# Projecting keys and values of all batches in a stage of their own, and stacking the halves of two heads in 64 rows each by the loads

## The reference, cut to what matters

```python
q = x @ Wq.T + bq;  k = context @ Wk.T + bk;  v = context @ Wv.T + bv     # 256 columns = 16 heads of 16
attn = softmax(einsum('bihd,bjhd->bhij', q, k) * 16 ** -0.5)              # 112 queries, 375 keys
out = einsum('bhij,bjhd->bihd', attn, v).reshape(B, NQ, 256)
return out @ Wo.T + bo
```

## Time and profile before

| | us |
|---|---|
| median of 3 runs (lowest to highest) | 3871.93 (3871.74 to 3872.47) |
| the profiled execution | 3868.77 |
| its span | 3867.0 |
| PE busy | 3016.1 (78%) |
| VectorE, ScalarE, POOL busy | 1709.9, 1316.2, 905.7 |

### The profile page before, as it was taken

How to read it: one execution, slowest core, us unless ns; L and a number is a source line. 1 busy time by engine, 2 the same in 40 slices (tenths; PEclk the granted TensorE clock), 3 DMA queues, 4 the chain that set the end, 5 groups by cost and what they waited for, 6 DMA issues and landing times. The chain is left out here.

```text
span 3867.0 us, 59553 instructions
## 1 busy us (share of the span) xinstructions
PE 3016.1 (78%) x19704; PEld 2381.5 (62%) x19704; DVE 1709.9 (44%) x3313; ACT 1316.2 (34%) x2657; POOL 905.7 (23%) x934
## 2 busy tenths in 40 slices
PE   4999929999999820999993588788888888709980
PEld 2666618777778710888882355466676667608870
DVE  2444467666667532000003444465655556502323
ACT  1222245555555300333330222344444445302220
POOL 0000004433334150000004100232323333160015
PEclk7999959999999755999996789899999999759995
DMA  4000000000000233565552000000000000035653
GB/s 109 1 1 0 0 9 13 14 13 16 13 14 13 96 102 97 170 199 190 182 199 88 19 0 0 12 13 14 10 13 10 13 7 13 1 92 182 202 171 113
DMA packets 174569, 234.68 MB, mean 61 GB/s; under 512 B 25184, under 2 KB 141376, under 8 KB 174384
## 3 DMA queue, kind: packets, MB, share of 16 engines
q1 hardware_dynamic: 156496, 184.23, 15.4%
q0 software_dynamic: 17888, 47.73, 3.7%
HBM read 186.04 MB, written 45.88 MB: 60 GB/s over the span
## 5 line engine op out<-in xcount | busy, mean ns | idle before, releaser
L1214 POOL TENSOR_TENSOR x_qH<-x_q_high,head_mask 128x448 fp32r<-128x448 f32 x256 | 277.0, 1082 | 1580.3 <-DVE x_q_low L1271 1246.4
L1284 DVE TENSOR_REDUCE x_neg_max<-banks 112x2 f32<-112x750 f32 x512 | 456.3, 933 | 259.7 <-PE banks L998 259.6
L1156 ACT ACTIVATE x_probT<-banks 125x448 f32<-125x448 f32 x768 | 417.1, 543 | 420.4 <-PE banks L1018 412.0
L1014 PE MATMUL banks<-x_qH,x_kS 128*125 128x448 f32 x768 | 383.5, 499 | 34.9 <-issue 32.4
L1734 PE MATMUL banks<-f_xT,f_w 128*128 128x256 f32 x1680 | 386.2, 385 | 17.6 <-DMA f_w<-in_L_ffn_w 12.9
L1746 PE MATMUL banks<-f_w,f_hT 128*128 128x256 f32 x1680 | 374.2, 379 | 0.0
L1734 PEld LDWEIGHTS banks<-f_xT,f_w 128*128 128x128 f32 x1680 | 319.6, 192 | 76.3 <-issue 23.2
L1746 PEld LDWEIGHTS banks<-f_w,f_hT 128*128 128x128 f32 x1680 | 313.9, 190 | 39.9
L1018 PE MATMUL banks<-x_diag,x_ones 112*125 112x448 f32 x768 | 288.9, 376 | 0.0
L1016 PE MATMUL banks<-x_qL,x_kS 128*125 128x448 f32 x768 | 288.2, 375 | 0.0
L970 PE MATMUL banks<-x_ctxT,x_wk 128*128 128x375 f32 x512 | 203.7, 522 | 83.0 <-DVE x_o L1302 79.9
(11 more groups left out here) (271 smaller groups left out, 4989.0 us busy)
## 6 DMA issues: line engine op xcount, KB each, us to landing
f_w<-in_L_ffn_w SPq DMA_DIRECT2D x70, 1024.0 KB, 8.3
f_w<-in_L_ffn_w SPq DMA_DIRECT2D x70, 512.0 KB, 5.0
f_x_slots<-slot_x SPq DMA_DIRECT2D x70, 256.0 KB, 6.0
slot_y<-f_y POOLq DMA_DIRECT2D x70, 256.0 KB, 5.5
f_ctx_rows<-in_ctx SPq DMA_DIRECT2D x32, 281.2 KB
x_cnat<-in_ctx SPq DMA_DIRECT2D x32, 281.2 KB
slot_x<-f_zero SPq DMA_DIRECT2D x10, 896.0 KB, 11.6
x_ctxT<-in_ctx_T SPq DMA_DIRECT2D x32, 187.5 KB
```

Source lines behind the costliest of these rows:

```text
L1014: pe.matmul(to, kS[:, r, q, keys], qH[:, r, heads, :].rearrange("p h t -> p (h t)"), start=True, stop=False)
L1156: act.activation(probT[:, u % 2, c].rearrange("k h t -> k (h t)"), ST[i % 2][0:KB, 0:HU * T], ACT.Exp).then_inc(exp_done, 1)
L1214: pool.tensor_tensor(qH[:, r, to, :], wide(q_high[:, q:q + 1, :], 1, HU), mask, ALU.mult).then_inc(qH_ready, 1)
L1284: dve.tensor_reduce(mx[:, u % 2, 2 * pair:2 * pair + 2], psum[0:T, 2 * pair:2 * pair + 2, 0:NKV], AX_X, ALU.max, negate=True).then_inc(max ...
```

## The change

There are eight stages: before each cross attention a new `project_context(e, layer)` goes through all batches, makes the keys and the value rows, and stores them in DRAM (`k_halves`: per batch, head half and high or low part, 128 rows of 376; `v_rows`: per batch 125 rows of 1536). In it each slot pair of batches has its own buffers, keys are cut straight out of PSUM by ScalarE (high) and VectorE (rest), and SP issues, in order, two stores of one batch and the load of another. The columns of the weights are reordered so that a head's 16 numbers come as rows `d * 8 + pair`.

In the cross attention two heads now share the 128 rows, 64 each: `kP` has for a head pair, per head, high, low, high, low of 16 rows each, and `qP` high, high, low, low against it, with zeros in the other head's 64 rows (zeroed once). So one pass gives all four products of the parts, and the masks of POOL and the second tile of queries are gone. The stacking is done by the loads: `load_keys` issues four DMAs a batch (two halves of the pairs x two heads), each reading 32 rows twice (`wide(..., 0, 2)`) into 64 partitions; the query parts are stored to DRAM (`store_query`) and read back by `load_query` with four DMAs, each 16 rows twice into 32 partitions. `load_values` reads the value rows. An exponent is the matmul of ones with the diagonal (448 columns) and one matmul a head pair (224 columns). Scores run two units ahead instead of one, one pair in each of a unit's first two slots, and the query is made two batches ahead.

```diff
+        env.k_halves = nc.dram_tensor("k_halves", [B, 2, 2, P, NKV + 1], F32, kind="Internal").ap()
+        env.v_rows = nc.dram_tensor("v_rows", [B, KB, NJ * XH * P // XU], F32, kind="Internal").ap()
+        env.q_halves = nc.dram_tensor("q_halves", [2, 2, 2, P, T], F32, kind="Internal").ap()
-        stages = [self_attention, lambda e: cross_attention(e, 0), lambda e: experts(e, 0),
-                  gated_attention, lambda e: cross_attention(e, 1), lambda e: experts(e, 1)]
+        stages = [self_attention, lambda e: project_context(e, 0), lambda e: cross_attention(e, 0),
+                  lambda e: experts(e, 0), gated_attention, lambda e: project_context(e, 1),
+                  lambda e: cross_attention(e, 1), lambda e: experts(e, 1)]
...
+def project_context(e, layer):
...
+                def load(b, i, r):
+                    if layer == 0:
+                        sp.wait_ge(v2_ps, ONE + least(i * 2 + r - 1))
+                        sp.dma_start(ctxT[:, r, 0, :], d["ctx_T"][0:P, bass.ds(b, 1), :].rearrange(
+                            "c b k -> c (b k)")).then_inc(ctx_loaded[r], 16)
+                        sp.dma_start(ctxT[0:C1, r, 1, :], d["ctx_T"][P:DC, bass.ds(b, 1), :].rearrange(
+                            "c b k -> c (b k)")).then_inc(ctx_loaded[r], 16)
+                    else:
+                        sp.wait_ge(cT_ps, ONE + least(i * 4 + 2 * r - 2))
+                        sp.dma_start(cnat[:, r, :, 0:DC], d["ctx_768"][bass.ds(b, 1)].rearrange(
+                            "b (j p) c -> p (b j) c", p=KB)).then_inc(ctx_loaded[r], 16)
...
+                def store(b, i, r):
+                    sp.wait_ge(k_low, ONE + i * 4 + 2 * r + 2)
+                    sp.dma_start(e.k_halves[bass.ds(b, 1)].rearrange("b h l p n -> p (b h l) n"),
+                                 halves[:, r].rearrange("p h l n -> p (h l) n").bitcast(F32)).then_inc(k_stored[r], 16)
+                    sp.wait_ge(v01_ready, ONE + i * 2 + r + 1)
+                    sp.wait_ge(v2_ready, ONE + i * 2 + r + 1)
+                    sp.dma_start(e.v_rows[bass.ds(b, 1)].rearrange("b p n -> p (b n)"),
+                                 v[:, r].rearrange("p c h e -> p (c h e)")).then_inc(v_stored[r], 16)
...
+                with sp.Fori(1, B // 2) as i:
+                    for r in range(2):
+                        store(i * 2 + r - 2, i - 1, r)
+                        load(i * 2 + r, i, r)
...
+    AHEAD = 2
+    RING = 4
+    AT = {"xT": 1, "q": 2, "back": 4, "oT": 7, "y": 8}
...
+                def load_keys(g, s):
...
+                    sp.wait_ge(st_ps, ONE + since(g, NU * NJ, SS * (s - 1)))
+                    parts = e.k_halves[bass.ds(b, 1)].rearrange("b h l (d p) n -> (b h) (l d) (p n)", d=HD)
+                    for half in range(2):
+                        pairs = slice(half * PAIRS // 2, (half + 1) * PAIRS // 2)
+                        keys = slice(pairs.start * (NKV + 1), pairs.stop * (NKV + 1))
+                        for h in range(2):
+                            sp.dma_start(kP[h * HALF:(h + 1) * HALF, r, pairs, :].bitcast(F32),
+                                         wide(parts[h:h + 1, :, keys], 0, 2)).then_inc(k_loaded[half][r], 16)
...
+                def load_query(g, s):
+                    r = s % 2
+                    sp.wait_ge(q_stored[r], g * (8 * GROUP) + 16 * (s // 2 + 1))
+                    parts = e.q_halves[r].rearrange("h l (d p) t -> h l d (p t)", d=HD)
+                    for h in range(2):
+                        for l in range(2):
+                            at = h * HALF + 2 * l * HD
+                            sp.dma_start(qP[at:at + 2 * HD, r, h].rearrange("q p t -> q (p t)").bitcast(F32),
+                                         wide(parts[h, l:l + 1], 0, 2)).then_inc(q_loaded[r], 16)
...
+                        if s < GROUP - 1 or not last:
+                            load_keys(g, s + 1)
+                            load_query(g, s + 1)
+                            load_values(g, s + 1)
+                        if s < GROUP - 2 or not last:
+                            store_query(g, s + 2)
...
-                    pe.matmul(to, kS[:, r, q, keys], qH[:, r, heads, :].rearrange("p h t -> p (h t)"),
-                              start=True, stop=False)
-                    pe.matmul(to, kS[:, r, q, keys], qL[:, r, heads, :].rearrange("p h t -> p (h t)"),
-                              start=False, stop=False)
-                    pe.matmul(to, ones[:], diag[:, u % 2].rearrange("t h k -> t (h k)"), start=False, stop=True)\
-                      .then_inc(st_ps, 1)
+                    pe.matmul(to, ones[:], diag[:, u % RING].rearrange("t h k -> t (h k)"), start=True, stop=False)
+                    for pair in range(2):
+                        last = pe.matmul(to[:, 2 * pair * T:2 * (pair + 1) * T].rearrange("k (h t) -> k h t", t=T),
+                                         kP[:, r, 2 * q + pair, keys],
+                                         qP[:, r, :, 2 * q + pair, :],
+                                         start=False, stop=(pair == 1))
+                    last.then_inc(st_ps, 1)
...
-                        if c == 0 and (u + 1 < NU or not last):
-                            score(g, u + 1, 0)
-                            score(g, u + 1, 1)
+                        if c < 2 and (u + AHEAD < NU or not last):
+                            score(g, u + AHEAD, c)
```

More of the change, by code:

```diff
@@ new lines, in group @@
+                def group(g, is_first, last):
+                    for s in range(GROUP):
+                        if s < GROUP - 1 or not last:
[4 more added lines that the diff above has]
+                            store_query(g, s + 2)
+                load_keys(0, 0)
+                load_values(0, 0)
+                store_query(0, 0)
@@ L1179, in group @@
                         j = SLOT.get(at)
-                        if j in MAKE and (s < GROUP - 1 or not last):
-                            copies(g, s + 1, j)
-                        for k in HIGH:
-                            if at == HIGH[k] and (s < GROUP - 1 or not last):
-                                high(g, s + 1, k)
-                        if j == "oT" and (s >= 1 or not is_first):
+                        if j == "xT" and (s < GROUP - 2 or not last):
+                            copy_xT(g, s + 2)
+                        if j == "oT" and layer == 0 and (s >= 1 or not is_first):
                             copy_oT(g, s - 1)
@@ L1191, in group @@
                             copy_oT(g, GROUP - 1)
-                if layer == 0:
-                    act.wait_ge(e.later, e.later_n)
-                for j in MAKE:
-                    copies(0, 0, j)
-                    if j in HIGH:
-                        high(0, 0, j)
+                for s in range(2):
+                    copy_xT(0, s)
                 all_groups(act, group)
@@ L1221, in group @@
                 def group(g, is_first, last):
-                    for s in range(GROUP - 1 if last else GROUP):
-                        spread(g, s + 1)
-                spread(0, 0)
+                    for s in range(GROUP - 2 if last else GROUP):
+                        add_post(g, s + 2)
+                add_post(0, 0)
+                add_post(0, 1)
                 all_groups(pool, group)
@@ L1340, in group @@
                                 normalise(g, s - 1)
[L1341 removed]
+                            if j == "y" and layer == 0:
                                 add_y(g, s - 1)
```

604 lines of the change are left out of this document (310 added, 294 removed).

## The result

| | us |
|---|---|
| kernel before, median (lowest to highest) | 3872.2 (3871.74 to 3872.59) |
| changed kernel, median (lowest to highest) | 6284.1 (6280.64 to 6292.77) |
| ratio (95% interval) | 1.623 (1.620 to 1.626) |
| span of the profiled execution of the changed kernel | 6282.2 |

The account below looks back on a forecast made before the run. PE's instruction stream was taken to bound both cross attentions before, and loads on two engines after. 2223 us kept, 766 of projection and 3164 of attention gave 6153 us of span, rounded to 6160 us measured, range 5750 to 6780.

Parts of the forecast that it names:

- Two engines for eight transfers: Cross attention: all eight key and query loads, leading count 2, run on the same two engines, 38.3 us a batch.
- rival of sixteen engines: Cross attention: the copies use all sixteen engines, 4.8 us a transfer, some 16 us a batch, 4110 us in all; chance 6%.
- Where the transfer lies: Cross attention: loads hide behind two units only; PE's work behind the wait adds 8.5 us a batch (layer 0), 7 (layer 1).
- The size of the transfer: Cross attention: a batch's key and query loads take 2.5 us of latency plus 38.3 us for 2.00 MB.
- Projection: New projection stages: 10.5 us a batch in layer 0 and 12.5 in layer 1, 766 us in all.
- the chain: Projection stages: PE, evictions, issue, values, load and latency in order over two batches, 8.2 to 10.9 us a batch.
- Work removed from PE: Cross attention: of PE's 23.0 us a batch 14.4 stay in layer 0, of 26.7 in layer 1 15.0 stay.
- A pass of 224 columns: Exponents of cross attention: each narrower PE pass takes 0.11 us; the rival at the upper bound had 1%.
- The rest: Everything outside the projection and cross attention stages: 2223 us stay of the 3867.0 us span.
- faster: Copies and value rows both spread over all engines: attention at 14.4 and 15.0 us a batch, 3754 us; chance 4%.
- no change: Whole kernel: the faster case with 16 us a batch of attention and 530 us of projection, 3867 us; chance 2%.
- The other signs: Attention: some 50 GB/s, PE busy about a quarter, period 48 to 50 us, longest waits on `qP`, clock near 0.6.

Follow-up runs that it names:

- copies_inside: Changed kernel with the copy loads' repeat moved inside the rows for keys, and query loads reading high and low once: ratio 1.056, 4161.5 us.
- values_128: Changed kernel with value rows padded by three rows of zeros, stored and loaded as 128 rows instead of 125: ratio 1.579, 6218.4 us.
- queries_sooner: spread_all with loads issued in another order, keys of a batch's first two units, queries, then keys of its last two: ratio 0.953, 3689.8 us.
- spread_all: Changed kernel with both the repeat moved inside, as in copies_inside, and the value rows padded to 128: ratio 1.032, 3999.5 us.
- keys_full_width: spread_all with the keys of both heads of a pair loaded by one transfer of 128 rows instead of two of 64: ratio 0.977.
- full_width_sooner: queries_sooner with the keys also loaded as 128 rows per transfer: ratio 0.945, and 0.952 (3685.3 us) when repeated on another chip.

## Why the prediction was right, and where its terms were off

The stages, from their first to their last instruction in the trace, against the sum: attention 1703 + 1670 = 3374 us (predicted 3164), projection 305 + 400 = 705 (766), the rest 2203 (2223). Three errors of +210, -61 and -20 leave 6282 instead of 6153. The mechanism was right; that the sum came within 2.1% of the span is in part luck: of the 210 us that the attention took more, 81 were taken back by the projection and the rest.

- **Two engines for eight transfers.** Right: share 0.16 with values and queries in it, 58 GB/s in both attentions, 52 to 53 where only the copies run, so 26 an engine, as taken. copies_inside, which moves one dimension, takes about a third off the time. The rival of sixteen engines (4110 us) is what the kernel becomes with that edit: its 4161.5 us, less the 50 us by which `experts(e, 0)` is longer on its chip, are about 4110. That this meets the rival's figure is luck: the periods are 18.5 and 17.9 us, not 16, at 236 GB/s for the keys where 418 was taken, and a cheaper projection makes up for it.
- **Where the transfer lies.** Right: 8.4 us of work behind the wait in the batch shown, 8.5 predicted for layer 0. Over 30 batches of each attention it is 7.8 us on average in layer 0 and 7.0 in layer 1, where 7 were taken.
- **The size of the transfer.** The term mis-sized: 2.5 + 38.3 = 40.8 us were taken and 45.3 measured in the batch shown. The packets of the trace take it apart, again over 30 batches: 1.7 us from SyncE's issue to the first packet of the keys, 33.6 for the keys, 9.1 for the queries, and 0.6 to PE's start. The first and the last together are 2.3 us for the 2.5 taken; the middle two are 42.7 for the 38.3. Over all batches the periods are 3.1 and 3.9 us above the 49.3 and 47.8 of the sum, 32 x 7.0 = 224 us, which is the +210 but for the edges; in layer 0 the work behind the wait, 0.7 us less than taken, hides a part of the excess. The start behind a pause makes most of it: the key packets take 229 ns when they run undisturbed, 128 of them to an engine 29.3 us, and by the windows 8 us at 32 GB/s instead of 52 are 3.1 us lost. It was not in the rows of before, where no transfer writes with two engines 32 partitions apart.
- **Projection.** 9.0 and 11.8 us a batch for 10.5 and 12.5. The engines' 8.8 us had been worked out, and then the chain was put on top with a clock between the levels. In layer 0 the chain is hidden: by values_128 the bound was the engines alone. The share of 0.58 and the 9.0 us in layer 0 lie outside the 0.3 to 0.5 and the 10 to 13 us that were to show it.
- **Work removed from PE.** 14.4 and 15.0 us were to stay. The changed kernel can't show it, queries_sooner does: 14.3 and 13.6 us, at clock 1.00 (a third of the value rows was read as 0.97 us and entered as 0.9, which is 0.2 us a batch; the 1.4 us that layer 1 came out lower was not followed up). So the gain that the change is after is real, 38 and 49% off the attention's period, and was buried under the loads. Of the whole kernel 5% is left, as the projection stages take some 530 us of it back.
- **A pass of 224 columns.** 0.11 us holds. Timeline of the changed kernel, at clock 1.00:

```profile
1300.40 0.37 PE L1182 MATMUL banks<-x_diag,x_ones 112*125 112x448 f32 x1
1300.61 0.38 PE L1184 MATMUL banks<-x_qP,x_kP 128*125 128x224 f32 x2
1300.82 0.50 PE L1168 MATMUL banks<-x_kP,x_qP 128*112 128x376 f32 x2
```

  Two passes go from 1300.61 to 1300.82, 0.105 us each.
- **The rest.** Self attention's last product lies 12.6 us earlier than before, and nothing of that stage was changed. The loads at the start were: `wq` takes one issue instead of four in either layer, the biases one instead of two or four, and SyncE's last issue ends at 36.1 us instead of 48.7. That was not in the sum. Before and after:

```profile
484.67 0.42 DVE L696 TENSOR_TENSOR sa_y<-banks,w_bo 112x256 f32<-112x256 f32 x1 [2.11 <-PE banks L558]
```

```profile
472.04 0.42 DVE L680 TENSOR_TENSOR sa_y<-banks,w_bo 112x256 f32<-112x256 f32 x1 [2.11 <-PE banks L542]
```

- **The rivals.** The point from which *faster* decides was put at a period of 16.5 us, or 5.5 us for the 2.00 MB of copies. It was well placed: spread_all, with 19.4 and 18.2 us, is at 1.032, as 64 partitions take only 200 to 240 GB/s; keys_full_width, with 16.2 and 15.4, is at 0.977. The sum of *no change* does not hold as it stands: it takes 530 us for the projection where *faster*, on which it builds, has 495; with 495 it is 3832 us, 0.9% less than before. And an order of loads (queries_sooner) crosses the point without a faster transfer. The sum didn't see that, as it put all eight transfers ahead of the wait though half the keys are needed two units later.
- **The other signs.** PE busy 0.30 of the attention ("about a quarter"), clock 0.64 and 0.63 ("near 0.6"), POOL 21 us of 1500, longest waits on `qP`: as written. The period was to be 48 to 50 and is 52.

## What to carry to other kernels

Read the leading count of both sides of every transfer before its bytes: 2 means two engines and 125 means five, and moving the repeat inside the rows costs nothing. Adding three rows of zeros gave 152 us in the two projection stages and lengthened the attention's period by 0.3 to 1.2 us, so such a padding wants a look at every stage that uses the tensor. Then look at the width (a destination of 64 partitions gets half the rate of one of 128) and at what is needed first: loads put in the order of need were worth 8% here, more than the 5% from the faster transfer. A DMA share of n/16 that stays flat while one load runs alone names the number of engines that carry it. And compare versions on one chip: a ratio to the kernel before, taken on another chip, was off by up to an estimated 0.016 here, a third of an effect of 0.045.

## What the hardware showed that was not expected

- Two engines writing 32 partitions apart start at 29 to 33 GB/s together, 64 or 16 apart at 44 to 48; all reach 53. The first pair reaches it once its packets start half a packet (0.11 us) apart.
- SyncE is held in the issue itself while transfers pile up: 19.6 us for the four query transfers on two engines, 2.5 us for the same bytes on sixteen.
- A wait of PE of 3.3 us in each batch costs 5.1: in the batch shown the granted clock is 0.50 over the 4 us behind it.
- The chips differ by 1.7% in the time of the kernel before (3872 or 3874, and 3939 or 3940 us), by 0.9% in that of full_width_sooner. Two versions compared across them seemed 0.8% apart that on one chip are 0.2% apart.
